# ScalarE's key casts in other places, value weights and context 2 loaded by need, the last scan block weighted in halves

## The reference

```python
x = x + _L0_xattn_ref(_layernorm(x), ctx_768, ...)   # cross attention, 16 heads of 16
x = x + _L0_attn_ref(_layernorm(x), ...)             # state-space scans (mamba)
x = x + _L0_ffn_ref(...)                             # attention and 8 experts
x = x + _L1_xattn_ref(_layernorm(x), ctx_768, ...)   # cross attention again
x = x + _L1_attn_ref(...); x = x + _L1_ffn_ref(...)

# cross attention: 128 queries against a context of 12544 x 192
q = (query @ Wq + bq); k = (key_value @ Wk + bk); v = (key_value @ Wv + bv)
attn = softmax(clip(q k^T * scale)); out = (attn @ v) @ Wo + bo
```

## Time and profile before

| what | value |
|---|---|
| median of 3 runs | 1217.75 us (1213.6 to 1218.22) |
| profiled execution: its own time | 1217.7 us |
| its span, first to last instruction | 1215.8 us |
| granted TensorE clock, mean | 0.972 |
| TensorE busy | 1113.9 us, 92% |
| VectorE busy | 720.4 us, 59% |
| ScalarE busy | 707.4 us, 58% |
| GpSimd busy | 208.8 us, 17% |
| chain that ended last | PE 64%, DVE 17%, ACT 11%, issue 4%, DMA 3% |

### The profile page before, as it was taken

One profiled execution on the slowest core, in us unless ns is written; L12 is line 12 of the kernel. 1 busy time (PEld: TensorE's weight loads), 2 busy tenths in 40 slices (PEclk: granted clock), 3 DMA queues, 4 the chain that ended last, 5 costly groups with the idle time before them and its releaser, 6 DMA issues.

```text
span 1215.8 us, 30429 instructions
## 1 busy us (share of the span) xinstructions
PE 1113.9 (92%) x12991; PEld 732.4 (60%) x12991; DVE 720.4 (59%) x1356; ACT 707.4 (58%) x1387; POOL 208.8 (17%) x126
## 2 busy tenths in 40 slices
PE   7899999999999999716799999999999999999777
PEld 4456666666666656616697456666566666666565
DVE  3776666666665664588323676656665666674343
ACT  4476666676766658352213466667676676677321
POOL 1231221222221200000001332222222211210000
PEclk9999999999999989858999999999999999999889
DMA  9764444554443360530832954444443444350540
GB/s 207 159 161 120 111 104 119 123 123 97 117 106 102 78 180 3 187 126 1 309 98 56 203 139 106 123 123 113 102 114 102 100 123 120 80 152 3 215 158 5
DMA packets 82904, 144.92 MB, mean 119 GB/s; under 512 B 10056, under 2 KB 72400, under 8 KB 82256
## 3 DMA queue, kind: packets, MB, share of 16 engines
q1 hardware_dynamic: 81488, 142.06, 44.4%
q0 software_dynamic: 384, 0.79, 0.4%
q10 hardware_dynamic: 896, 0.12, 0.1%
HBM read 64.64 MB, written 0.15 MB: 53 GB/s over the span
## 4 chain that ended last, share of the span: by engine, by line
PE 64%; DVE 17%; ACT 11%; issue 4%; DMA 3%; SPq 1%; ACTq 0%; DVEq 0%
PE ring L584 35%; PE st L584 16%; PE ot L584 12%; DVE mpart L1318 7%; ACT work L1054 5%; DVE arena L1457 1%; ACT arena L1019 1%; ACT arena L1030 1%; ACT work L1060 1%; DVE work L1342 1%; DMA warena<-ctxT 1%; SPq L407 1%; DVE work L1338 1%; DMA qst<-rowb 1%; DMA arena<-rows 1%
## 5 line engine op out<-in xcount | busy, mean ns | idle before, releaser
L1318 DVE TENSOR_REDUCE mpart<-ring 128x1 f32<-128x448 f32 x896 | 529.9, 621 | 306.1 <-PE ring L584 301.6
L1054 ACT ACTIVATE work<-st 128x512 f32<-128x512 f32 x784 | 407.1, 603 | 97.3 <-PE st L584 96.5
L584 PE MATMUL ring<-arena,qst 96*128 96x448 bf16 x896 | 284.8, 358 | 4.6 <-DVE mpart L1318 3.9
L584 PE MATMUL st<-qst,arena 97*128 97x128 bf16 x3136 | 241.5, 220 | 4.2 <-DMA qst<-rowb 3.0
L584 PE MATMUL ot<-work,arena 128*17 128x128 f32 x6272 | 235.4, 276 | 7.4 <-issue 0.8
L584 PEld LDWEIGHTS st<-qst,arena 97*128 97x128 bf16 x3136 | 206.9, 98 | 45.6 <-ACT work L1054 6.3
L541 POOL TENSOR_TENSOR arena<-arena 128x896 f32<-128x896 f32 x52 | 98.1, 1886 | 563.6 <-ACT arena L1026 563.4
L584 PEld LDWEIGHTS ot<-work,arena 128*17 128x17 f32 x6272 | 143.7, 97 | 81.0 <-ACT work L1054 37.9
L584 PEld LDWEIGHTS ring<-arena,qst 96*128 96x128 bf16 x896 | 79.9, 98 | 112.8 <-issue 73.2
L584 PE MATMUL ring<-wkv,warena 128*128 128x256 f32 (+1 forms) x616 | 124.9, 400 | 2.4
L584 PE MATMUL ring<-warena,wkv 64*128 64x448 f32 (+1 forms) x352 | 119.8, 576 | 0.6 <-DVE mpart L1318 0.6
(11 more groups left out here) (285 smaller groups left out, 774.3 us busy)
## 6 DMA issues: line engine op xcount, KB each, us to landing
arena<-arena SPq DMA_DIRECT2D x336, 224.0 KB, 3.8
arena<-ffn_W SPq DMA_DIRECT2D x16, 1024.0 KB, 13.1
warena<-ctxT SPq DMA_DIRECT2D x60, 224.0 KB, 4.7
warena<-ctxT SPq DMA_DIRECT2D x26, 448.0 KB, 3.9
arena<-f SPq DMA_DIRECT2D x2, 4096.0 KB, 25.0
arena<-scratch_bc SPq DMA_DIRECT2D x1, 2048.0 KB, 6.7
arena<-rows SPq DMA_DIRECT2D x1, 1792.0 KB, 7.1
wkv<-L_wkv SPq DMA_DIRECT2D x8, 128.0 KB, 5.7
```

What stands on the lines that cost most here:

```text
L584: return nc.tensor.matmul(o, l, r, start=start, stop=stop, **kw)
L1054: nc.scalar.activation(pbuf[:, n % 2, half * 512:(half + 1) * 512], st[:, 2 * (n % 2) + half], ACT.Exp).then_inc(*signal(f"{lay}_exp_done"))
L1318: V.reduce_max(mpart[:, 2 * h + hf:2 * h + hf + 1], ring[:, BANKS[step][0], 0:HALF], AX_X).then_inc(*signal(f"{lay}_b_max"))
```

## The change

- `schedule()`: the casts of the keys of chunk c + 3 stand elsewhere. k1 of the first half goes from pair 4 of chunk c to pair 5, ahead of the second key projection's copies; k2 of the first half from pair 5 of chunk c to pair 0 of chunk c + 1, ahead of the value projection's copies; k1 of the second half from pair 6 of chunk c to the same place; k2 of the second half from pair 0 of chunk c + 1 to pair 2, ahead of the copies. TensorE's and VectorE's order stays as it was in these chunks.
- Six reductions instead of four stand ahead of the first scores of each attention, and pairs 0 and 3 of chunk 0 have one fewer each.
- GpSimd does rest(0), third(0), rest(1), third(1) from chunk 3 on; the copy of projected keys waits for k3 of its own half.
- `stack` is split by halves on SP's queue; for chunk 0 the loads of context 2 stand between the halves.
- The main part of the value weights signals a semaphore of its own, and the first value projection waits for it instead of the second key matmul.
- The last scan block's product is done in two instructions of 1024 elements, each with a signal, and TensorE starts on the first 8 states after the first.

```diff
@@ -139,12 +139,12 @@
     for kind, k in (("k", 0), ("k", 2), ("v", 0)):
         plan += some(3, 0) + [(kind, 2, k)] + some(3, 0) + [(kind, 2, k + 1)]
     plan += some(2, 0) + pair("v", 2, 2) + [("row", 0, 0)]
-    plan += some(4, 1) + score(0) + some(1, 1) + score(1) + some(2, 1)
+    plan += some(6, 1) + score(0) + some(1, 1) + score(1) + some(2, 1)
 
     values = {0: (0, 1), 2: (2, 3)}
     keys = {3: (0, 1), 5: (2, 3)}
     for c in range(NCH):
-        per_pair = ((7, 6, 6, 6, 4) if c == 0 else (5, 4, 5, 5, 4)) + (5, 4)
+        per_pair = ((6, 6, 6, 5, 4) if c == 0 else (5, 4, 5, 5, 4)) + (5, 4)
         for w in range(UNITS // 2):
             if w == 5 and c + 1 < NCH:
                 plan.append(("row", c + 1, 0))
@@ -157,6 +157,10 @@
             plan += some(1, limit) + score(c * UNITS + 2 * w + 2) + (sums[1:] if single else [])
             plan += some(1, limit) + score(c * UNITS + 2 * w + 3)
             plan += some(n - 2 - made, limit)
+            if c and w in values and c + 2 < NCH:
+                plan += [("k2", c + 2, 0), ("k1", c + 2, 1)] if w == 0 else [("k2", c + 2, 1)]
+            if w == 5 and c + 3 < NCH:
+                plan.append(("k1", c + 3, 0))
             if w in values and 0 < c < NCH - 2:
                 plan += [("v", c + 2, k) for k in values[w]]
             if w in keys and c + 3 < NCH:
@@ -166,10 +170,6 @@
                 plan.append(("o", c - 1, 0))
             if c == 0 and w < 3:
                 plan += ([("k1", 2, 0), ("k1", 2, 1)], [("k2", 2, 0)], [("k2", 2, 1)])[w]
-            if c and w == 0 and c + 2 < NCH:
-                plan.append(("k2", c + 2, 1))
-            if c + 3 < NCH and w >= 4:
-                plan.append((("k1", c + 3, 0), ("k2", c + 3, 0), ("k1", c + 3, 1))[w - 4])
     assert not maxima
     return plan + [("o", NCH - 1, 0)]
 
@@ -423,7 +423,7 @@
                          f"{lay}_wkv_in")
 
             def value_weights(lay):
-                load(wkv[:, 0, 1], a[f"{lay}_wkv"][1, 0:P], f"{lay}_wkv_in")
+                load(wkv[:, 0, 1], a[f"{lay}_wkv"][1, 0:P], f"{lay}_wv_in")
 
             def first_ctx(lay):
 
@@ -440,27 +440,27 @@
                     load(ctxt[part * TAIL:(part + 1) * TAIL, par, 1], a["ctxT"][P:CC, at:at + CK],
                          f"{lay}_ctx_in{par}")
 
-            def stack(lay, c):
+            def stack(lay, c, m):
 
                 b = c % KBUFS
-                if c >= KBUFS:
+                if c >= KBUFS and m == 0:
                     sp.wait_ge(sem(f"{lay}_s_full"), 2 * (c - KBUFS + 1) * UNITS)
-                for m in range(KC):
-                    for part in range(3):
-                        sp.wait_ge(sem(f"{lay}_k{part + 1}_done"), KC * c + m + 1)
-                        for s in range(SLOTS):
-                            if K_SPLIT[s] == part:
-                                load(kst[s:SLOTS * HD:SLOTS, b].rearrange("l (h m) k -> l h m k", m=KC)[:, :, m],
-                                     kparts[:, part, m * CK:(m + 1) * CK], f"{lay}_kst{m}_in")
+                for part in range(3):
+                    sp.wait_ge(sem(f"{lay}_k{part + 1}_done"), KC * c + m + 1)
+                    for s in range(SLOTS):
+                        if K_SPLIT[s] == part:
+                            load(kst[s:SLOTS * HD:SLOTS, b].rearrange("l (h m) k -> l h m k", m=KC)[:, :, m],
+                                 kparts[:, part, m * CK:(m + 1) * CK], f"{lay}_kst{m}_in")
 
             def attention_loads(lay, later_weights):
                 sp.wait_ge(sem(f"{lay}_ones_set"), 1)
                 load(arena[STACKED:STACKED + 1, A_KST:A_V].rearrange("p (n k) -> p n k", k=HALF), ones, f"{lay}_ones_in")
                 for c in range(NCH):
-                    stack(lay, c)
-                    if c + 2 < NCH:
-                        sp.wait_ge(sem(f"{lay}_v_full"), 4 * (c + 1))
-                        load_ctx(lay, c % 2, (c + 2) * CK)
+                    for m in range(KC):
+                        stack(lay, c, m)
+                        if m == min(c, 1) and c + 2 < NCH:
+                            sp.wait_ge(sem(f"{lay}_v_full"), 4 * (c + 1))
+                            load_ctx(lay, c % 2, (c + 2) * CK)
                 sp.wait_ge(sem(f"{lay}_v_full"), 4 * NCH)
                 later_weights()
 
@@ -553,8 +553,11 @@
                 def split(c):
                     for m in range(KC):
                         rest(c, m)
-                    for m in range(KC):
-                        third(c, m)
+                        if c > 2:
+                            third(c, m)
+                    if c <= 2:
+                        for m in range(KC):
+                            third(c, m)
 
 
                 nc.gpsimd.memset(ones, PAIR_OF_ONES).then_inc(*signal(f"{lay}_ones_set"))
@@ -650,7 +653,7 @@
                     if (c, n) == (0, 0):
                         pe.wait_ge(sem(f"{lay}_first_in"), 16 * FIRST_LOADS)
                     if (c, n) == (0, 1):
-                        pe.wait_ge(sem(f"{lay}_wkv_in"), 16 * PROJECTION_LOADS)
+                        pe.wait_ge(sem(f"{lay}_wkv_in"), 16 * KC)
                     if (c, n) == (0, 1) or (c and n == 0):
                         pe.wait_ge(sem(f"{lay}_ctx_in{c % 2}"), 16 * PROJECTION_LOADS * (c // 2 + 1))
                     mm(SPOT[BANKS["k", c, n][0]][:, 0:HALF], wkv[:, 0, 0, m * P:(m + 1) * P],
@@ -688,6 +691,8 @@
                     if kind == "k" and (c, n // 2) != (0, 0):
                         keys(c, n)
                     if kind == "v":
+                        if (c, n) == (0, 0):
+                            pe.wait_ge(sem(f"{lay}_wv_in"), 16)
                         for t in range(2 * n, min(2 * n + 2, TPC)):
                             mm(SPOT[bank][:, (t % 2) * D:(t % 2 + 1) * D], ctxt[:, c % 2, 0, t * P:(t + 1) * P],
                                wkv[:, 0, 1], start=(t % 2 == 0), stop=False, skip_group_check=True)
@@ -782,6 +787,8 @@
                         keep_clock(14, 6)
                     pe.wait_ge(sem("weighted"), b + 1)
                     for n in range(NS):
+                        if (b, n) == (NB - 1, NS // 2):
+                            pe.wait_ge(sem("weighted"), NB + 1)
                         last = mm(pb[2 + 2 * (b % 2)][:, 0:TOK], ident, m_hc[:, b % 2, n * TOK:(n + 1) * TOK],
                                   start=(n == 0), stop=(n == NS - 1))
                     last.then_inc(sem("summed"), 1)
@@ -1013,8 +1020,8 @@
                         preload(ACT.Exp)
                     if kind == "k":
                         m, hf = n // 2, n % 2
-                        if n == 0 and c:
-                            act.wait_ge(sem(f"{lay}_k3_done"), KC * c)
+                        if hf == 0 and c:
+                            act.wait_ge(sem(f"{lay}_k3_done"), KC * (c - 1) + m + 1)
                         act.wait_ge(sem(f"{lay}_k_full"), 4 * c + n + 1)
                         nc.scalar.activation(ktf[:, m * CK + hf * HALF:m * CK + (hf + 1) * HALF],
                                              SPOT[BANKS[step][0]][:, 0:HALF], ACT.Identity, bias=bk[:, m:m + 1]
@@ -1458,8 +1465,11 @@
                                          ALU.add).then_inc(*signal("scanned"))
                     dve.wait_ge(sem("scanned"), b + 1)
 
-                    V.tensor_tensor(m_hc[:, b % 2], m_["h"], m_["bc"][:, NS * TOK:], ALU.mult
-                                    ).then_inc(sem("weighted"), 1)
+                    for lo, n in ((0, NS),) if b + 1 < NB else ((0, NS // 2), (NS // 2, NS // 2)):
+                        at = slice(lo * TOK, (lo + n) * TOK)
+                        V.tensor_tensor(m_hc[:, b % 2, at], m_["h"][:, at],
+                                        m_["bc"][:, (NS + lo) * TOK:(NS + lo + n) * TOK], ALU.mult
+                                        ).then_inc(sem("weighted"), 1)
                     if b + 1 < NB:
                         inputs(b + 1)
                     dve.wait_ge(sem("weighted"), b + 1)
```

## The result

| | before | after |
|---|---|---|
| median | 1217.3 us (1213.6 to 1218.22, 4 runs) | 1201.01 us (1195.62 to 1203.22, 4 runs) |
| span of the profiled execution | 1215.8 us | 1199.2 us |
| TensorE busy | 1113.9 us | 1105.2 us |
| ScalarE busy | 707.4 us | 714.8 us |

The ratio is 0.9863, with an interval of 0.984 to 0.9885: 1.4% faster, 16.3 us. The forecast was 1207.0 with a range of 1199 to 1213, so the sign and the range held, and the gain was 5.6 us larger than the 10.65 of the sum.

The account below looks back on a forecast made before the run. TensorE was taken to bound both attentions, busy 32.84 of a chunk's 33.26 us. Gains of 14.25 us less losses of 3.6 gave 10.65, so 1217.7 would become 1207.0 us, range 1199 to 1213.

Parts of the forecast that it names:

- Part 1: Chunk boundaries: moving key casts starts the exponentials 0.49 us earlier at 22 boundaries, a gain of 10.8 us.
- Rival D: Chunk boundaries: nothing is won because the context copy or the scores bind earlier; 1218 us, chance 0.09.
- rivals B and E: Boundaries: first, the whole bubble goes, 1199 us, chance 0.07; second, casts overrun the value copies, 1229 us, chance 0.03.
- Part 2: Late row, next stage's weights: the row lands later behind later weights, losing 1.6 us in layer 0, 1.4 in layer 1.
- Rival A: Late row: it doesn't queue behind the weights, so the 3.0 us loss falls away; 1204 us, chance 0.20.
- Part 3: Start, second key matmul: no longer waiting for the value weights gains 0.1 us, bounds 0 and 0.3.
- Part 4: Context 2 ahead of the stack's second half: wait handed on, gain 0; gaps before first row cost 0.3 us per layer.
- Part 5: Chunk 0 of each attention: two reductions moved ahead of the first scores gain 2.3 us in all, bounds 1.2 and 2.4.
- Part 6: Scan tail: halving the last product lets TensorE start at 573.0 instead of 574.09, a gain of 1.05 us.
- Rival C: Late row or first row: new stalls lower TensorE's clock and context 2 costs 1.5 us; 1212 us, chance 0.15.

Follow-up runs that it names:

- a_k2back: Kernel after, with only the first half's k2 cast put back between the key copies and the copy of the finished context: 1219.53 us, one run.
- p4_ctx2: Kernel before, with only the loads of context 2 moved between the halves of chunk 0's stack: 1220.93 us, one run.
- p5_reds: Kernel before, with only two more reductions ahead of the first scores and one fewer in pairs 0 and 3: 1213.95 us, one run.
- p1_casts: Kernel before, with only the moved key casts, GpSimd's new order and the key copies' wait by halves: 1203.62 us, ratio 0.9882, 4 runs.
- p6_halves: Kernel before, with only the last scan block's product done in two halves: 1213.13 us, one run.
- a_noctx2: Kernel after, with context 2's loads again behind the whole stack of chunk 0: 1200.24 us, ratio 0.9861.
- a_rowfirst: Kernel after, with SyncE waiting for chunk 13's row transfer before issuing the next stage's weights: 1196.85 us, ratio 0.9832.

## Why the prediction was right and wrong

- **Part 1, right.** 0.49 us a boundary was forecast; the distances give 0.51 (one in layer 1 gives 0.23, the same one in every kernel with the moved casts; its cause is open), 9.9 for 20 of them, where 9.8 was forecast; the other two lie in the first stretch of each layer. What was said to be late next, exponentials 0.49 behind their scores, stands in the timeline (0.48), and so does SP's delay (1.66, forecast 1.6). The margin is 0.47, a little over the forecast 0.25 to 0.4, and the boundary's context matmuls take 1.45, where "near 1.3" was named as a sign. a_k2back, one run with 20 like distances, shows that the gain is this one cast. Rival D, that nothing is won, and rivals B and E fall with it.
- **Part 2, right in layer 1, wrong in layer 0.** Layer 1 lost 1.65 us (forecast 1.4). In layer 0 the forecast was a loss of 1.6, and it won 3.41. The step that failed is that the row lands as the weights run out and so goes 1.6 us later with them. The reading behind it, "its 32 packets move only in 446 to 448 us, as the weights run out", is right for the kernel before; in the kernel after the packets move with 0.63 MB of the weights still to come. Of the 3.41, 0.56 are shorter idle; the rest is the clock, which fell behind the 2.10 us before and not behind the 1.54 now. Most of this gain is luck: behind longer waits (2.36 and 2.19 us) the clock held in other runs. Rival A had 2.1 us and none for the two waits; they are 1.54 and 1.52.
- **Part 3** was put at 0.1, bounds 0 and 0.3: TensorE's start at 11.56 didn't move, and the context ends the wait as foreseen (1.37 us of idle, released by the DMA of `ctxT`). The value weights were not run alone.
- **Part 4, right near 38 us, too cheap at the first row.** Handing on the wait came out (39.74, forecast 39.6 to 39.71; in p4_ctx2 39.23). The gaps before the first row were charged 0.3 in layer 0; the runs show 0.9 to 3.4 (3.6 if a_k2back is held against p5_reds), because the row lands 1.0 us later behind its issue and the clock can fall behind the wait. The bound of 2 for both layers was too low for the worst case. It is a cost that the part has, and no gain stands against it.
- **Part 5, right in layer 0** (1.1). In layer 1 it gave 2.4, as it also keeps the clock: of four kernels without the early reductions (before, p1_casts, p4_ctx2, p6_halves) three lost it there, of the eight with them none. The sum of the layers was put at 2.3 and is 3.5 alone.
- **Part 6** was put at 1.05 and gave 0.37 in this kernel. The step that failed is "TensorE starts at 573.0": the matmuls of `keep_clock` weren't counted as work ahead of it. It gives 0.05 to 0.6 behind a slow sum and 1.07 behind a quick one.
- **What no step held**: 2.2 us of the last stage, whose code is the same. There 20 matmuls of the `ring` take 2.50 us where they took 4.13, 32 of `st` 3.84 where they took 5.46, and 8 of `st` 3.36 where they took 2.27; the clock falls at other places. This accounts for the stretch's difference in kind; it wasn't put to a test. p1_casts has 1.3 of it and p5_reds 2.4, whose edits don't reach this stage, while p4_ctx2 and p6_halves have none. So it can come without the change; whether it is chance isn't shown.

Stretch by stretch against the forecast (minus is faster than forecast): start of layer 0 +2.0 (+0.57 where -1.15 for the reductions, -0.49 for the cast, -0.1 and +0.3 were forecast); the 20 distances -0.1 and chunk 10 to 11 +0.1; late row of layer 0 -5.0, of layer 1 +0.25; scans +0.7 (-0.37 for -1.05); start of layer 1 -1.7 (of it 1.2 the clock); last stage -2.2. These sum to -5.95, which is the difference (16.6 of the span less 10.65). So the size was missed by clock and waits at five places, not at the boundaries, and that the total came within 5.6 us of the sum is in part luck: misses of +2.0 and +0.7 stand against -5.0, -2.2 and -1.7. Rival C had the right mechanism, stall and clock, with the wrong sign.

Two of the prediction's own sums don't come out. Rival C's terms (2.6 for the clock, 1.5 for part 4 where 0.6 was counted) give 1210.5 and not 1212. The chances of forecast, A, B and half of C add to 0.805 and not 0.83, those of D and the other half of C to 0.165 and not 0.14. Neither changes the forecast.

**A better version.** a_both, the kernel after without part 4 and with the rows ahead of the weights, ran at 1194.71 us, 6.3 below the change. The intervals of the two ratios overlap (0.9804 to 0.9851 and 0.984 to 0.9885), so the difference isn't shown by the time alone, but the stretches are shorter by 1.7, 1.7 and 2.1 us at the places of the two edits, and the weights' later start made no new wait.

**Open** stays what decides whether the clock falls at a wait, what packet by packet holds the row behind earlier weights, and what adds 1.0 us behind the last packet of chunk 0's row when SP's queue has been busy ahead of it.

## What to carry to other kernels

When one engine is busy 98% of a stage, look at what stands between its last matmul and its next one on the other engines: work that nobody needs soon, ahead of a copy in an in-order engine, is paid at every turn (here 0.5 to 0.6 us of a cast of 0.94), and moved into a gap it cost nothing. For each DMA that an engine waits for, ask what was issued ahead of it on the other queues, and issue the small urgent one first. A bulk load started 1.6 us later changed the time from the row's issue to its landing by +1.7 us in one layer (3.7 to 5.4) and by -0.6 in the other (6.0 to 5.4). Count keep-alive matmuls as work when what follows them is made earlier.

## What the hardware showed beside this

- The 4 KB DMA of the late row on ScalarE's queue takes 1.6 to 1.7 us (2.2 in one of eight cases) when it is issued ahead of the weights on SP's, and 3.4 to 6.4 behind them, on another queue though it is.
- The fall of the clock isn't decided by the length of the idle alone. Behind waits at the late row it fell after 2.10, 2.52 and 2.59 us (before, p4_ctx2, p5_reds), not after 2.36 and 2.19 (p6_halves, a_noctx2); it fell two us after waits of 1.78 and 1.51 (p1_casts), and not after 1.54 and 1.52 (after); at the first scores it fell after 0.81 (after) and not after 0.84 (a_rowfirst) or 0.93 (before); behind the same 1.14 us in layer 1 it fell in two kernels (before, p4_ctx2) and held in one (p6_halves). A fall costs 1.2 to 3 us. So one run of a small part can't be told from the clock's share: p6_halves was 4.6 us faster with an edit that gave 0.6 there.
